# The product with V in pairs of steps instead of fours, and the numerators of the last stage loaded a chunk ahead

## The reference

```python
xn = _layernorm(x)
c_q, c_kv = xn @ Wq_down, xn @ Wkv_down
q_c, k_c, v_c = heads(c_q @ Wq_up), heads(c_kv @ Wk_up), heads(c_kv @ Wv_up)
q_r, k_r = heads(xn @ Wq_rope), xn @ Wk_rope
attn = softmax((q_c k_c^T + q_r k_r^T) / sqrt(HEAD_DIM + ROPE))
s = (attn @ v_c) @ Wo
g = silu(ffn(xn))     # ffn: w2(silu(w1 xn) * (w3 xn)), each with its low-rank part
out = x + s * g
```

## Time and profile before

| | us |
|---|---|
| median of 3 runs | 2015.23 |
| lowest and highest | 2010.91, 2015.40 |
| the profiled execution | 2011.28 |
| its span | 2009.50 |
| mean granted PE clock | 0.985 of full |

### The profile page before, as it was taken

The page is one execution under the profiler, slowest core; times in us unless marked ns, Lnnn a source line. Parts: engine busy times, 40 slices in busy tenths (PEclk is TensorE's granted clock), DMA queues, the critical chain, the costliest instruction groups (busy, mean ns, idle before and its releaser), DMA issues.

```text
span 2009.5 us, 40807 instructions
## 1 busy us (share of the span) xinstructions
PE 1853.8 (92%) x12538; PEld 1482.1 (74%) x12538; DVE 1517.5 (76%) x1510; ACT 1410.7 (70%) x1884; POOL 1325.9 (66%) x1342
## 2 busy tenths in 40 slices
PE   8899999999999999999999999999999998888887
PEld 6677877777777777777777787777777777656665
DVE  8577787778778777877787878777777887665555
ACT  5557787777777878787877788887777776542222
POOL 5208787878777877778787878787877774032443
PEclk9999999999999999999999999999999999989888
DMA  8744444444444444444444444444444444463441
GB/s 252 218 93 104 99 108 98 102 106 102 105 106 104 101 103 98 107 96 108 97 110 95 112 97 109 97 106 97 106 99 100 107 105 112 111 170 116 137 126 63
DMA packets 186535, 225.22 MB, mean 112 GB/s; under 512 B 59710, under 2 KB 113758, under 8 KB 186462
## 3 DMA queue, kind: packets, MB, share of 16 engines
q1 hardware_dynamic: 182374, 223.52, 46.9%
q10 hardware_dynamic: 4112, 1.08, 0.3%
HBM read 61.26 MB, written 35.65 MB: 48 GB/s over the span
## 4 chain that ended last, share of the span: by engine, by line
PE 53%; DVE 14%; DMA 11%; issue 11%; ACT 5%; SPq 3%; POOL 2%; DVEq 0%; ACTq 0%; POOLq 0%
PE st L1115 14%; PE pj L1149 12%; DMA slot<-mrow 8%; PE sx L1128 7%; PE ob L1149 7%; PE ob L1081 6%; DVE pw L1019 4%; DVE mx L1026 3%; DVE slot L1037 3%; PE ap L1854 2%; ACT slot L933 1%; DMA x_raw_h<-o_scratch 1%; ACT pf L992 1%; DVE kc L1014 1%; POOL num L1515 1%
## 5 line engine op out<-in xcount | busy, mean ns | idle before, releaser
L850 POOL TENSOR_TENSOR pw<-pf,pw 128x1024 f16<-128x1024 f32 x348 | 805.6, 2330 | 306.3 <-ACT pw L1001 285.4
L1026 DVE TENSOR_REDUCE mx<-sx 128x4 fp32r<-128x1024 f32 x512 | 626.8, 1224 | 328.1 <-PE sx L1128 323.0
L992 ACT ACTIVATE pf<-st 128x1024 f32<-128x1024 f32 x464 | 446.4, 1011 | 30.8 <-PE st L1115 29.1
L1115 PE MATMUL st<-slot,k 128*128 128x512 f32 x1024 | 415.9, 406 | 45.4 <-DMA slot<-mrow 37.9
L1001 ACT ACTIVATE pw<-pf 128x1024 f16<-128x1024 f32 x348 | 355.3, 1053 | 112.1 <-PE ob L1081 99.2
L1115 PE MATMUL st<-slot,krlh 128*128 128x512 f32 x1024 | 402.7, 393 | 0.0
L1128 PEld LDWEIGHTS sx<-k,slot 88*128 88x128 f32 x2048 | 314.2, 190 | 70.9 <-issue 20.2
L1128 PE MATMUL sx<-k,slot 88*128 88x256 f32 x2048 | 332.4, 285 | 19.3 <-DMA slot<-kc 9.9
L1115 PEld LDWEIGHTS st<-slot,k 128*128 128x128 f32 x1024 | 193.2, 189 | 111.1 <-issue 71.5
L1019 DVE TENSOR_TENSOR pw<-pf,pw 128x1024 f16<-128x1024 f32 x116 | 228.2, 1967 | 1.8
L1115 PEld LDWEIGHTS st<-slot,krlh 128*128 128x128 f32 x1024 | 193.8, 189 | 35.6
(11 more groups left out here) (244 smaller groups left out, 2499.0 us busy)
## 6 DMA issues: line engine op xcount, KB each, us to landing
slot<-slot SPq DMA_DIRECT2D x256, 256.0 KB, 3.1
k<-kc SPq DMA_DIRECT2D x256, 128.0 KB
w_stage<-in_Wq_rope SPq DMA_DIRECT2D x64, 256.0 KB, 4.8
o_scratch<-o_sb SPq DMA_DIRECT2D x256, 64.0 KB
c_scratch<-stage SPq DMA_DIRECT2D x32, 256.0 KB, 3.2
c_in<-c_scratch SPq DMA_DIRECT2D x128, 64.0 KB, 2.3
k<-kc SPq DMA_DIRECT2D x128, 48.0 KB
k<-kx SPq DMA_DIRECT2D x128, 48.0 KB
```

Of the source, the lines that this page charges most:

```text
L850: nc.gpsimd.tensor_tensor(pw[:, s, kt, 1], pf[:, 2 * odd + kt], pw[:, s, kt, 0], ALU.subtract).then_inc(lo_done[kt][odd], 1)
L992: nc.scalar.activation(dst, st[:, kt], ACT.Exp, scale=SCALE).then_inc(exp_done, 1)
L1026: nc.vector.tensor_reduce(mx[:, p, lo:lo + 4], sx[:, :, :].rearrange("p a (b k) -> p (a b) k", b=2), axis=AX.X, op=ALU.max).then_inc(red_d ...
L1115: last = nc.tensor.matmul(st[:, kt, h, :].rearrange("p (e n) -> p e n", e=PH), kk, q[:, s, :, h, :], start=(n == 0), stop=(n == 1))
```

## The change

In attention, the product with V of two steps runs in every even step, directly behind the first half of the row scores, ahead of `project`; it waits for the remainders of steps seven and eight back. ACT copies one half of `ob` out per product, and SP stores both its pieces in the following odd step. The row of maxima is written into the half of `ob` that the product doesn't use. DVE takes `remainder` between the two maxima of every even step, and `content_lo` at the start of the third step of a turn instead of inside the fourth. In even steps the second half of the row scores stands after 6 of 12 projection matmuls instead of after 9. POOL makes the V planes in the third step, and copies them to their places in the fourth. In the last stage, `output_hi` stands at m = 4 and 5 (before: 8 and 9) and `output_lo` at 5 and 6 (before: 9 and 10); the first six parts of the next chunk are loaded at the chunk's start, four of them into the tile `den`, and the denominators are spread into `den` after these are added; POOL normalises in the third and fourth tile of the chunk before. DVE no longer waits for all sums before it makes `b2`.

```diff
@@ -781,10 +791,10 @@
 
-            def store_o(at, k, pieces=(0, 1, 2, 3)):
-                bp = (k // NS) % NBP
+            def store_o(at, k):
+                bp, q = (k // NS) % NBP, (k // 2) % 2
                 g = at.g if k >= 0 else at.g - 1
-                hold(sp, passed, o_evac, at.turn(k) + 1)
-                for h, q in ((n // 2, n % 2) for n in pieces):
+                hold(sp, passed, o_evac, at.pair(k) + 1)
+                for h in range(2):
                     b = 2 * bp + h
                     sp.dma_start(o_dram[bass.ds(g, 1), :, q, :, b * S:(b + 1) * S].rearrange("a e p n -> (a e) p n"),
-                                 o_sb[64 * h:64 * h + 64, q, :]).then_inc(o_stored, 16)
+                                 o_sb[64 * h:64 * h + 64, q, :]).then_inc(o_stored[q], 16)
 
...
@@ -810,6 +820,6 @@
                 if at.last and k > STEPS:
-                    if k in (STEPS + 1, STEPS + 6):
-                        store_o(at, k - 6 if k == STEPS + 1 else k - 7)
-                elif k % NS and at.live(k - k % NS - 5):
-                    store_o(at, k - k % NS - 5, ((), (0,), (1, 2), (3,))[k % NS])
+                    if k < STEPS + 5:
+                        store_o(at, 2 * k - 26)
+                elif k % 2 and at.live(k - 9):
+                    store_o(at, k - 9)
                 if not at.last:
...
@@ -836,7 +846,8 @@
                     kk = k - 4
-                    if at.split(kk):
-                        if s == 1:
-                            planes(at, kk - 1)
-                    else:
+                    if not at.split(kk):
                         whole(at, kk)
+                if s == 2 and at.live(k - 6) and at.split(k - 6):
+                    planes(at, k - 6)
+                if s == 3 and at.live(k - 7) and at.split(k - 7):
+                    kept_planes(at, k - 7)
                 if at.live(k - 4) and at.split(k - 4):
...
@@ -959,11 +973,11 @@
                     exponentials(at, k - 4, 1)
-                    if at.split(k - 4):
-                        rounded(at, k - 4)
+                if ending:
+                    if k < STEPS + 4:
+                        evacuate(at, 2 * k - 24)
+                elif k % 2 == 0 and at.live(k - 8):
+                    evacuate(at, k - 8)
+                if at.live(k - 4) and k - 4 < STEPS and at.split(k - 4):
+                    rounded(at, k - 4)
                 if s == (2 if at.first and k < NS else 1) and k < STEPS and at.live(k + NS):
                     content_hi(k // NS + 1, at.turn(k) + 1)
-                if s == 0 and at.live(k - 5):
-                    act.wait_ge(av_done, at.step(k) - 4)
-                    if at.live(k - 5 - NS):
-                        act.wait_ge(o_stored, 64 * at.turn(k - 5))
-                    nc.scalar.activation(o_sb[:, :, :], ob[:, :, :], ACT.Copy).then_inc(o_evac, 1)
                 if k in (13, 14, 15) and not at.last:
...
@@ -973,2 +987,10 @@
 
+            def evacuate(at, k):
+
+                q = (k // 2) % 2
+                act.wait_ge(av_done, at.step(k) + 2)
+                if at.live(k - NS):
+                    act.wait_ge(o_stored[q], 32 * at.turn(k))
+                nc.scalar.activation(o_sb[:, q, :], ob[:, q, :], ACT.Copy).then_inc(o_evac, 1)
+
             def max_row(at, k, row):
...
@@ -1030,4 +1052,4 @@
                 split = k % 2 == 0 and at.live(k - 5) and at.split(k - 5)
-                if split and k % NS == 0:
-                    remainder(at, k - 5)
+                if k % NS == (3 if at.first and k < NS else 2) and k < STEPS and at.live(k - k % NS + NS):
+                    content_lo(k // NS + 1, at.turn(k) + 1)
                 if at.live(k - 1) and k <= STEPS:
...
@@ -1045,6 +1067,4 @@
                     maxima(at, k - 1, 0)
-                    if split and k % NS == 2:
+                    if split:
                         remainder(at, k - 5)
-                    if k % NS == 3 and k < STEPS and at.live(k + 1):
-                        content_lo(k // NS + 1, at.turn(k) + 1)
                     maxima(at, k - 1, 1)
...
@@ -1054,18 +1074,25 @@
         def tensor(pe, head, tail):
-            def values(at, k, steps=1):
+            def product(at, k):
 
 
-                s, v = k % NS, at.step(k)
-                if steps:
-                    pe.wait_ge(exp_done, 2 * (v + steps))
-                    pe.wait_ge(vx_ready, v + steps)
-                    if at.split(k):
-                        for done in lo_done[0] + lo_done[1]:
-                            pe.wait_ge(done, at.pairs(k + steps - 1))
+                v = at.step(k)
+                pe.wait_ge(exp_done, 2 * (v + 2))
+                if at.split(k):
+                    pe.wait_ge(vx_ready, NS * (at.turn(k) + 1))
+                    for done in lo_done[0] + lo_done[1]:
+                        pe.wait_ge(done, at.pairs(k))
+                else:
+                    pe.wait_ge(vx_ready, v + 2)
                 if at.first and k == 0:
                     pe.wait_ge(vx_filled, FILLS)
-                if at.last and k == 3 * NS:
-                    pe.wait_ge(o_evac, at.turn(k))
-                elif s == 0:
+                if at.last and k > 2 * NS:
+                    pe.wait_ge(o_evac, at.pair(k))
+                else:
                     pe.wait_ge(ql_done, 2 * v + 4 * NS)
+                for i in range(2):
+                    values(at, k + i)
+
+            def values(at, k):
+
+                s = k % NS
                 for kt in range(2):
...
@@ -1089,4 +1116,4 @@
                 pe.wait_ge(red_done, 2 * at.step(k) + 4)
-                if k % NS and k < 3 * NS and (k > NS or not at.first):
-                    pe.wait_ge(o_evac, at.turn(k))
+                if not (at.last and k + 3 > STEPS) and at.live(k - 6):
+                    pe.wait_ge(o_evac, at.pair(k - 6) + 1)
                 if at.first and k == 0:
...
@@ -1143,5 +1170,3 @@
                 for c in range(KD):
-                    if c == 2 and k % NS == 0 and at.live(k - 2 * NS) and at.split(k - 2 * NS):
-                        turn(at, k - 2 * NS)
-                    if c == KD - 1 and at.live(k - 1):
+                    if c == (KD - 1 if k % 2 or not at.live(k - 2 * NS) else KD - 2) and at.live(k - 1):
                         row_scores(at, k - 1, 1)
...
@@ -1167,11 +1192,6 @@
                     row_scores(at, k - 1, 0)
-                if k % NS == 0 and at.live(k - 2 * NS) and not at.split(k - 2 * NS):
-                    turn(at, k - 2 * NS)
+                if k % 2 == 0 and at.live(k - 2 * NS):
+                    product(at, k - 2 * NS)
                 project(at, k)
 
-            def turn(at, k):
-
-                for i in range(NS):
-                    values(at, k + i, 0 if i else NS)
-
             def drain(at, k):
...
@@ -1345,3 +1364,3 @@
 
-    x_tile, xl_tile = x_raw_h[:, 3, 3 * CH:], x_raw[:, 3, 3 * CH:]
+    x_tile = x_raw_h[:, 3, 3 * CH:]
 
...
@@ -1350,9 +1369,9 @@
 
+        if n < KD:
+            return den[:, n, :], part_loaded[0], KD * c + KD - 1
         if c == 0:
-            if n < KD:
-                return den[:, n, :], part_loaded[n], 0
-            return ((x_tile, part_loaded[KD], 0), (xl_tile, part_loaded[KD + 1], 0))[n % 2][:2] + ((n - KD) // 2,)
-        if n % 2:
-            return spare_tile[:, :], part_loaded[KD + 2], (c - 1) * KD + n // 2
-        return x_tile, part_loaded[KD], 2 + (c - 1) * KD + n // 2
+            tile = (0, 1, 2, 0)[n - KD]
+            return (x_tile, hh[:, 1, :].bitcast(F32), hh[:, 2, :].bitcast(F32))[tile], part_loaded[1 + tile], int(n == 2 * KD - 1)
+        i = n % 2
+        return (x_tile, spare_tile[:, :])[i], part_loaded[1 + 3 * i], (0 if i else 2) + 2 * (c - 1) + (n - KD) // 2
 
...
@@ -1360,3 +1379,5 @@
         tile, loaded, _ = num_part(c, n)
-        if n >= (KD + 2 if c == 0 else 2):
+        if c == 0 and n == 2 * KD - 1:
+            sp.wait_ge(num_done, KD + 1)
+        if c and n >= KD + 2:
             sp.wait_ge(num_done, c * 2 * KD + n - 1)
...
@@ -1452,5 +1477,6 @@
             if c + 1 < NC:
-                sp.wait_ge(r_stored, 16 * (c + 2))
                 sp.wait_ge(on_done, (c + 1) * KD)
-                spread_den(sp, c + 1)
+                for n in range(KD + 2):
+                    load_num_part(sp, c + 1, n)
+                sp.wait_ge(r_stored, 16 * (c + 2))
                 if c + 2 < NC:
...
@@ -1459,3 +1485,5 @@
                 load_num(sp, c + 1)
-                for n in range(2):
+                sp.wait_ge(num_done, (2 * c + 3) * KD)
+                spread_den(sp, c + 1)
+                for n in range(KD + 2, 2 * KD):
                     load_num_part(sp, c + 1, n)
...
@@ -1472,5 +1500,2 @@
                     load_xt(i + 2)
-                if c + 1 < NC and i + 1 < NI:
-                    for n in range(2 * i + 2, 2 * i + 4):
-                        load_num_part(sp, c + 1, n)
                 if i == 1 and c + 2 < NC:
...
@@ -1525,3 +1551,3 @@
```

(62 more changed lines are left out.)

6 lines of the change are left out of this document (3 added, 3 removed).

## The result

The changed kernel takes 2041.34 us (median of 4 runs, 2036.0 to 2046.91). In the same comparison the kernel before takes 2013.07 (2009.93 to 2015.4). The ratio is 1.0142, 95% interval 1.0108 to 1.0175: slower by 28 us, where 1972 was forecast. Its profiled execution took 2042.96 us with a span of 2041.1, against 2011.3 and 2009.5.

The account below looks back on a forecast made before the run. PE's order and its waits were taken to bound the kernel. From 2011.3, less 10 for the loop, plus 3 for first and last groups, less 33 for the last stage: 1971, stated as 1972, range 1948 to 2008 (8 in 10).

Parts of the forecast that it names:

- The second block: Attention loop: two V blocks of 32 cost 2.32 us instead of 1.96 for one, making PE's work 24.78 us a turn.
- The waits that go: Attention loop: PE no longer waits for the row of maxima (landing 1.8 us), the first step's V block or the transpose.
- the row of maxima stays slow: Rival, chance 0.12: in both odd steps the row lands late, each pair of steps waits 0.7 us, 2051 in all.
- The wait that comes, t: Third step: PE waits about t, the time of `content_lo` on DVE; 1.3 us, 1.7 in the fourth turn, mean 1.4.
- 24.78 + 1.4 = 26.18: Attention loop: PE's work plus the new wait gives 26.18 us a turn against 26.36, 10 us less over 57 turns.
- SP late with the content: Attention loop: an unpriced wait that would upset the whole, SP's stores now standing ahead of the next turn's loads.
- The clock: Last stage: low clock after PE's four stands made the restarts' matmuls take 8.5 us more, counted in the gain there.
- The last stage: PE's 32.6 us of stands for `ol` and 8.5 of low clock go, 2.0 a chunk stays: 33 us less, bounds 25 and 41.
- The numerators: Last stage, rival, chance 0.12: a late product of POOL holds ACT's `output_hi` at m = 4; 17 us back, 1988.
- First and last groups: Attention's first and last groups: little to remove, and the new wait comes three times or so, 3 us more.

Follow-up runs that it names:

- `store_step1`: The changed kernel with the stores of the group's last odd step issued behind the next group's first load of content: 2010.91 us, ratio 0.9978.
- `both`: `lo_step4` and `store_step1` together: 1934.74 us, ratio 0.9621.
- `only_content_first`: The changed kernel with SP issuing the load of content ahead of the loads of V and of the next content in each first step: 1980.23 us, ratio 0.9843.
- `tail_only`: The kernel before with the last stage of the changed kernel and nothing else of it: 1987.61 us, ratio 0.9853.
- `lo_twice`: The changed kernel with `content_lo` done twice: 2160.92 us, ratio 1.0732.
- `lo_step4`: The changed kernel with `content_lo` moved one step on, to the head of the fourth step: 1932.37 us, ratio 0.9578.

## Why the prediction was wrong

**The second block: nearly right.** Two steps with a product and two with a transpose take 24.86 us without waits; I had 24.78.

**The waits that go: right.** The row of maxima landed after 1.8 us behind three of four transposes near 1030, and after 2.9 behind the fourth, below the 4.2 from which it costs. The first step's product and the transpose wait for nothing. The rival "the row of maxima stays slow" did not come; `store_step1` and `both` show that it was near, since moved stores bring it back.

**The wait that comes, t: right on average.** 1.34 us a turn against 1.4. Three turns of a group have 1.0 to 1.3, and the fourth 2.1 where I had 1.7: the two errors cancel in the mean. The rule of the Trainium skill ("SBUF — State Buffer", "Who interferes with whom") held: the trace agrees, since `content_lo` starts at 1031.14, POOL's refill runs until 1032.38, and 1.24 + 1.08 make the 2.32. It holds the other way too: POOL's cast, 0.29 for the next pieces, took 1.29 behind it. Where the refill was moved, the long case went.

**What failed is the step on the loop: "24.78 + 1.4 = 26.18".** It took one wait as the only new one, at full clock. Measured is 27.26, 1.08 more, x 57 = 62 us, and that is nearly the whole miss (2041 - 1972 = 69). Over a group of four turns it is 4.3 us. Two things that were left out make 3.2 of them; the slightly longer block makes 0.3, and some 0.7 in small pieces have no cause shown.

- The order of SP. I weighed the stores against the row of maxima and not against what stands behind them on SP's own queue. I named "SP late with the content" as what would upset the whole and gave it no price, though the rows for one were there: 1.8 us for two stores, 0.65 for the weight load, 1.3 for V and the content. The slack was thin, and a wait of 1.5 to 1.7 us a group came of it. `only_content_first` takes this alone away and measures 1980.23 us, 8 above the forecast. It has 26.18 a turn in the group shown, as forecast, but that one group meets the sum by luck: the mean from 300 to 1600 is 26.24, 3 to 4 us more over 57 turns, and its last stage makes up the other 4 (182.1 us behind the start of the last product, 29 less than before and not 33).
- The clock. I priced low clock for the last stage, where I had rows of it, and none for the loop, where the waits of the kernel before, up to 1.8 us, had none behind them. About 1.5 us a group were lost to it, 20 us in all.

**The last stage: right in kind, its size too large.** 33 less was forecast with bounds 25 and 41; by the traces it is 29 alone (`tail_only`) and 25 in the changed kernel, where the last product's own half clock takes 1.1 of the rest. The stand for `ol` went, but 2.0 us a chunk were to stay, and near 4 did in the changed kernel: `hid`, then the sums and `z` on DVE and ACT, which now come late in place of `ol`, and some low clock behind `z`. The numerators came in time. That rival didn't come either.

**First and last groups.** 3 us more were forecast; about 6 is what is left of the 31.7 between the profiled executions after 51 for the loop and 25 for the last stage. The late denominators are in it.

## What to carry to other kernels

When stores or loads are regrouped, walk down their own issuing queue first: whatever stands behind them starts later, and the place to look is where a rare item, here a weight load once in four turns, falls on the same step. An operation that has slack of a whole turn belongs in the step where nobody waits for what stands behind it; here the same instruction cost 109 us ahead of a product and little one step on. Price waits together: the same edit was worth 61 us in one neighbourhood and 19 in another, and an edit that merely moves a transfer moved the wait with it.

## What the runs showed of the hardware

Ahead of a product, the granted clock fell to its lower level behind some waits of PE of 1.8 us and more, and not behind others of the same length: behind 31 of 51 in `lo_twice`, 5 of 14 in `store_step1`, 13 of 13 in the changed kernel. Each fall cost about 1.5 us in the changed kernel. In `lo_step4` it also fell behind a wait of 1.66 us for content.

A DVE operation with two inputs in SBUF and a POOL operation held each other off in both directions: `content_lo` took 2.32 us behind a POOL refill that had begun 0.05 us earlier, where it took 1.22 in half of the turns, and POOL's cast of 0.29 us took 1.29 behind `content_lo`.
